# Cross attention with routed expert blocks: second transposes at the head of the next step, reciprocals spread through memory, product on GpSimd

## The chip, the cores and the metric

The kernel runs on one core of one Trainium2 chip. The metric is the device time of one execution in microseconds, as the median of several executions. A core has TensorE (PE, with its weight loads as PEld), VectorE (DVE), ScalarE (ACT), GpSimd (POOL) and SyncE (SP), which here only issues DMAs. Each runs its own list of instructions in order. The lists meet at semaphores: an instruction waits until a count is reached, and everything behind it on its engine waits too.

## What is computed

x is 128 sequences of 64 tokens of width 128, ctx the same shape. Cut to what matters:

```python
q = split_heads(layernorm(x) @ Wq.T + bq)          # 16 heads of 8
k = split_heads(ctx @ Wk.T + bk); v = split_heads(ctx @ Wv.T + bv)
probs = softmax(q @ k.T / sqrt(8))                 # within a sequence: 64 x 64
x = x + merge_heads(probs @ v) @ Wo.T + bo
xf = layernorm(x)
e = argmax(xf @ Wr.T + br)                         # one of 8 experts for each token
h = relu(xf @ W1[e].T + b1[e])                     # 128 -> 512
out = x + h @ W2[e].T + b2[e]
```

## The kernel before

The 8192 tokens are 64 tiles of 128 (two sequences a tile), in 16 groups of four tiles. There are three stages.

Stage 1 loads x and ctx group by group, normalises, and makes Q, K and V with TensorE; Q and K are kept with channels in the partitions (QT, KT). For the scores, K must be laid out block-diagonally: KM holds, for one group, each head's 8 channels in its own column block, zeros elsewhere. SP fills it by 16 small DMAs a group (line 341), with a buffer for each of two groups; for group 0 GpSimd does (line 410).

Stage 2 is a hand-made pipeline of steps. Step n works on several tiles at once, each at another stage:

- TensorE: scores of tile n (L877, banks 0 to 3, two tiles in turn); transposes of the exponentials of tile n-2 in two halves (L918), both into bank 4, the second half after other work of the step; between them the spreading matmul of tile n-8 (L948), the output matmul of tile n-9 (L952), in even steps the router's logits (L959), in odd steps the transposes of two finished tiles of X (L977, bank 6); then, for tile n-3, probabilities times values (L994, into bank 6) and the softmax denominators (L1003, into bank 5, a group's four tiles in one area).
- VectorE: the routing operations of a batch of eight tiles in a few steps of eight (L655 to L690), maximum over the scores (L698), once in four steps the reciprocal of a group's denominators (L702), subtraction (L706), the product of numerators and spread reciprocals (L722), the residual (L725), statistics for the second layer norm (L735 and the lines 587 to 595).
- ScalarE: numerators of tile n-4 to NUM (L526), first half of PT (L529), X1T in odd steps (L535), second half of PT (L538), the exponential of tile n (L546).
- GpSimd: two masked copies of V, VP, for tile n-1 (L451), the inverse root by Newton steps for batches 0 to 5, and one indirect DMA a step that sends a finished tile's rows to its experts' places (L466).

The reciprocals of a group lie in one 128x128 tile RD. To multiply them with one tile's numerators they must be spread over the eight channels of each head; L948 does this by a matmul with a 0/1 matrix C_SEL, into bank 7, from where VectorE reads them. The semaphores that matter: pt_done and pt_ready (each half of the transposes, each copy), exp_done, x1t_ready, rd_done, ot_ready. The matmuls L994 wait for the X1T copy of their step, since that copy reads bank 6, which they write.

Stage 3 runs 71 blocks of 128 rows through their expert (L1009 to L1037 on TensorE) and sends the rows home by indirect DMAs (L473). It begins at step 67, beside the last steps of the pipeline, which run on to the end of the routing. SOON says how many steps earlier than the others the last two batches are routed; L_MUL and L_X1 are the steps by which the product and the residual stand behind the scores.

Of the kernel before, what the change touches and what calls it, by code (L numbers as in the profile page):

```python
# [14 lines left out]
P = 128  # L15
D = 128
SEQ = 64
BATCH = 128
TOK = BATCH * SEQ
NT = TOK // P  # L20
GT = 4
NG = NT // GT
GW = GT * P
H = 16
# [20 lines left out]
C_ID, C_TRI, C_ONE, C_OWN, C_DEN, C_SEL, C_PREF, C_BASE, C_LIM, C_BLK, C_EPS, C_1H, C_LE, C_END = np.cumsum(  # L45
    [0, P, P, P, 2 * DK, GT * 64, GT * P, E, E, NT, NB, 1, ST, E * E]).tolist()
# [5 lines left out]
def constants():  # L52
# [12 lines left out]
    for t in range(GT):  # L65
        c[:, C_SEL + P * t:C_SEL + P * (t + 1)] = (p[:, None] // DK == p[None, :] // DK) & (p[:, None] % DK == t)
# [16 lines left out]
L_MUL = 8  # L83
L_X1 = 9
# [14 lines left out]
SOON = 2  # L99
# [67 lines left out]
def build(nc, x, ctxT, wts, we, w2, con, pad, ids, out):  # L167
# [3 lines left out]
    rows = nc.dram_tensor("rows", (ROWS, RW), f32).ap()  # L171

    ctx = ExitStack()
    with ctx:
# [20 lines left out]
        BQK = W[:, W_BQ:W_BQ + 2]  # L195
        WR, BR = W[:, W_R:W_R + E], W[:, W_BR:W_BR + E]

        X1T = sb("X1T", P, 4, 2, P)
# [37 lines left out]
        RD = sb("RD", P, 2, P)  # L236
        OT = sb("OT", P, 2, P)
# [37 lines left out]
        con_in, w_in, ids_in, w2_in = sem("con_in"), sem("w_in"), sem("ids_in"), sem("w2_in")  # L275
# [15 lines left out]
        num_kept, rdx_done, wr_mm, wr_ready = (sem(n) for n in ("num_kept", "rdx_done", "wr_mm", "wr_ready"))  # L291
# [19 lines left out]
        def _(sp):  # L311

            def load_group(s):
                def go(before):
# [3 lines left out]
                    if isinstance(s.n, int) and s.n == 0:  # L318
                        sp.dma_start(C[:], con).then_inc(con_in, 16)
                        sp.dma_start(W[:], wts).then_inc(w_in, 16)  # L320
                        sp.dma_start(IDS[:], ids).then_inc(ids_in, 16)
# [10 lines left out]
            def spread(s):  # L332
                sp.wait_ge(q_kept, s.n + 1)
                sp.sem_inc(spread_go, 1)
                need(sp, s_done, GT * (s.n - 1))
                sp.sem_inc(spread_go, 1)
                at = bass.ds(s.n * GW, GW)
                for g in range(2):
                    for j in range(HP):
                        own = slice(SEQ * g + DK * j, SEQ * g + DK * (j + 1))  # L340
                        sp.dma_start(KM[own, s.r, j, :], KT[own, at]).then_inc(km_in[s.r], 16)
            steps(sp, 1, NG, 2, spread, peel=2)


            for r in range(2):
                sp.wait_ge(km_in[r], 16 * H * (NG // 2 - 1 + r))
            sp.dma_start(PADR[:], pad).then_inc(padr_in, 16)
            sp.dma_start(WE[:], we).then_inc(we_in, 16)
            sp.wait_ge(s_done, NT - GT)
            sp.dma_start(W2, w2).then_inc(w2_in, 16)  # L350
# [18 lines left out]
            for n in range(NB1 - E):  # L369
# [727 lines left out]
```

## Time and profile before

| | us |
|---|---|
| median of 3 executions | 499.29 (499.02 to 500.56) |
| the profiled execution | 501.58, its span 499.8 |
| TensorE busy (weight loads) | 461.1, 92% (347.9, 70%) |
| VectorE busy | 408.2, 82% |
| ScalarE busy | 313.0, 63% |
| GpSimd busy | 240.6, 48% |
| granted TensorE clock, mean | 0.982 |

The span is the time between the first and the last record of the execution; the rest of its 501.58 us lies around it. Busy time is work recorded on the engine, and says nothing of whether the work was on the path. TensorE's matmuls are pipelined, so a group's duration reaches beyond the start of the next one: the distance between starts is what a group takes in the queue. An idle time is put down to the releaser that the semaphores name.

### The profile page before, as it was taken

What the parts mean: (1) busy time and instruction counts of PE and PEld (TensorE: products, weight loads), DVE (VectorE), ACT (ScalarE), POOL (GpSimd) and SP (SyncE); (2) the same over time, 40 slices, a digit from 0 to 9 for tenths busy, and PEclk for the clock granted to TensorE, in tenths of its full rate; (3) what the DMA queues carried; (4) which work ended last, traced back from release to release, by engine and by line L of the source; (5) the groups of instructions that cost most, each with busy time, mean ns of one, the idle gap of its engine ahead of it and who ended that gap; (6) DMA issues with size and microseconds to landing.
All of it is one profiled execution on the core that took longest, in us unless ns stands there. A gap on an engine that the chain in (4) does not pass through costs nothing. (4 is left out here: it accounts for less than half of the span.)

```text
span 499.8 us, 18728 instructions
## 1 busy us (share of the span) xinstructions
PE 461.1 (92%) x6467; PEld 347.9 (70%) x6467; DVE 408.2 (82%) x1061; ACT 313.0 (63%) x589; POOL 240.6 (48%) x390
## 2 busy tenths in 40 slices
PE   3999978899999999999999999988789999999990
PEld 1666634456666666666666666668779999999990
DVE  4999864677899899998999999958878887887870
ACT  1677764666666666666666665665557777777760
POOL 1548620222232464555645645554767645455551
PEclk9999995999999999999999999999999999999996
DMA  8356300011000111111111115722223332222100
GB/s 281 108 148 177 90 11 12 14 22 20 18 17 18 33 41 30 38 38 36 35 34 33 39 41 201 264 71 76 77 66 103 101 87 66 72 61 74 39 32 0
DMA packets 32752, 33.98 MB, mean 68 GB/s; under 512 B 6675, under 2 KB 26006, under 8 KB 32416
## 3 DMA queue, kind: packets, MB, share of 16 engines
q1 hardware_dynamic: 27840, 24.10, 18.7%
q0 software_dynamic: 4832, 8.80, 5.3%
q8 instruction: 53, 0.87, 0.8%
q14 instruction: 27, 0.22, 0.2%
HBM read 19.14 MB, written 9.99 MB: 58 GB/s over the span
## 5 line engine op out<-in xcount | busy, mean ns | idle before, releaser
L451 POOL TENSOR_TENSOR VP<-BIG,C 128x128 f32<-128x128 f32 x128 | 56.1, 458 | 136.5 <-PE PS L1003 132.7
L918 PEld LDWEIGHTS PS<-C,SB 128*128 128x128 f32 x512 | 54.6, 142 | 68.2 <-ACT SB L546 32.5
L698 DVE TENSOR_REDUCE MX<-PS 128x16 f32<-128x1024 f32 x64 | 78.3, 1223 | 29.1 <-PE PS L877 27.7
L473 POOL DMA_INDIRECT out<-SB,BIG x71 | 70.1, 987 | 52.6 <-DVE SB L849 44.7
L918 PE MATMUL PS<-C,SB 128*128 128x128 f32 x512 | 85.1, 290 | 7.5 <-ACT PT L529 7.2
L546 ACT ACTIVATE SB<-SB 128x1024 f32<-128x1024 f32 x64 | 67.7, 1057 | 23.7 <-DVE SB L706 22.0
L706 DVE TENSOR_TENSOR SB<-PS,MX 128x1024 f32<-128x1024 f32 x64 | 77.4, 1210 | 1.7
L1024 PE MATMUL PS<-BIG,KM 128*128 128x128 f32 x568 | 76.8, 277 | 0.3 <-issue 0.2
L1037 PE MATMUL PS<-KM,SB 128*128 x568 | 75.8, 277 | 0.6 <-ACT SB L563 0.6
L466 POOL DMA_INDIRECT rows<-X,DESTI x64 | 64.2, 1003 | 19.6 <-issue 14.1
L877 PE MATMUL PS<-KM,BIG 64*64 64x512 f32 x512 | 71.2, 629 | 0.8 <-ACT BIG L517 0.8
L559 ACT COPY KM<-BIG 128x644 f32 x71 | 51.7, 729 | 30.2 <-PE PS L1024 24.8
L1024 PEld LDWEIGHTS PS<-BIG,KM 128*128 128x128 f32 x568 | 69.7, 192 | 1.4 <-issue 1.2
L1037 PEld LDWEIGHTS PS<-KM,SB 128*128 128x128 f32 x568 | 69.1, 192 | 1.2 <-issue 0.8
L538 ACT COPY PT<-PS 128x512 f32<-128x512 f32 x64 | 37.5, 586 | 36.7 <-PE PS L918 36.6
L529 ACT COPY PT<-PS 128x512 f32<-128x512 f32 x64 | 37.4, 585 | 36.2 <-PE PS L918 32.8
L838 DVE TENSOR_TENSOR SB<-PS,KM 128x512 f32<-128x512 f32 x71 | 49.0, 690 | 5.4 <-PE PS L1024 2.4
L563 ACT ACTIVATE SB<-SB 128x512 f32<-128x512 f32 x71 | 44.6, 628 | 10.0 <-DVE SB L838 9.7
L994 PE MATMUL PS<-PT,VP 128*32 128x64 f32 x2048 | 42.3, 223 | 0.2
L1003 PE MATMUL PS<-PT,C 128*32 128x128 f32 x1024 | 40.3, 276 | 1.1 <-DVE RD L702 0.7
L994 PEld LDWEIGHTS PS<-PT,VP 128*32 128x32 f32 x2048 | 31.9, 110 | 11.1 <-issue 11.0
L846 DVE TENSOR_TENSOR SB<-PS,KM 128x128 f32<-128x128 f32 x71 | 20.6, 291 | 18.1 <-PE PS L1037 17.2
(122 smaller groups left out, 699.0 us busy)
## 6 DMA issues: line engine op xcount, KB each, us to landing
BIG<-rows SPq DMA_DIRECT2D x71, 66.0 KB, 1.9
X<-in_x SPq DMA_DIRECT2D x16, 256.0 KB, 3.3
PT<-in_ctxT SPq DMA_DIRECT2D x16, 256.0 KB, 3.0
KM<-BIG SPq DMA_DIRECT2D x240, 16.0 KB
BIG<-in_we SPq DMA_DIRECT2D x1, 2576.0 KB, 11.5
KM<-in_w SPq DMA_DIRECT2D x1, 2048.0 KB, 15.9
out<-SB,BIG POOLq DMA_INDIRECT x71, 2.3
rows<-X,DESTI POOLq DMA_INDIRECT x64, 2.4
```

The source lines that it names most:

```text
L451: last = nc.gpsimd.tensor_tensor(dst, v, own, ALU.mult)
L466: nc.gpsimd.indirect_dma_start(out=rows, out_offset=bass.IndirectOffsetOnAxis(ap=DESTI[:, j % 2, t:t + 1], axis=0), in_=X[:, j * ST + t, : ...
L473: nc.gpsimd.indirect_dma_start(out=out, out_offset=bass.IndirectOffsetOnAxis(ap=RT[:, s.r, ID:ID + 1].bitcast(i32), axis=0), in_=YO[:, s.r ...
L546: nc.scalar.activation(SB[:, n % 3, :], SB[:, n % 3, :], ACT.Exp, scale=SCALE).then_inc(exp_done, 1)
L559: nc.scalar.copy(WS[:, s.r % 4, :], WE[:, bass.ds(ex, 1), :].rearrange("p e f -> p (e f)")).then_inc(ws_ready, 1)
L698: nc.vector.tensor_reduce(MX[:, n % 2, :], sc, axis=AX.X, op=ALU.max).then_inc(mx_done, 1)
L706: nc.vector.tensor_tensor(SB[:, n % 3].rearrange("p (h k) -> p h k", h=H), sc, MX[:, n % 2, :].unsqueeze(2).to_broadcast([P, H, SEQ]), ALU ...
L877: last = nc.tensor.matmul(bank(2 * (n % 2) + g)[SEQ * b:SEQ * (b + 1), :], QT[rows_g, n * P + SEQ * b:n * P + SEQ * (b + 1)], KM[rows_g, g ...
L918: last = nc.tensor.transpose(bank(4)[:, i * P:(i + 1) * P], SB[:, n % 3, hp * P:(hp + 1) * P], ident)
L994: nc.tensor.matmul(bank(6)[32 * c:32 * c + 32, at:at + SEQ], VP[:, m % 2, b, 2 * c + z, :], PT[:, m % 2, 2 * c + z, SEQ * b:SEQ * b + SEQ] ...
L1024: last = nc.tensor.matmul(bank(2 + b.r % 2)[:, c * P:(c + 1) * P], WS[:, b.r % 4, c * P:(c + 1) * P], XT[:, b.r % 2, :], start=True, stop= ...
L1037: last = nc.tensor.matmul(bank(4 + b.r % 2)[:, 0:D], HT[:, b.r % 2, c * P:(c + 1) * P], w, start=c == 0, stop=c == FC - 1)
```

## The change

Four things change in the steps, and some around them.

- The second half of a tile's transposes leaves step n (tile n-2) and stands at the head of step n+1, before the scores; ScalarE's copy of it moves to the head of its own step, before the numerators.
- The spreading matmul and C_SEL are gone. SP writes a group's reciprocals to memory (ratio) and reads them back spread over the partitions into RDX, both inside its loop over the groups, after the spreading of K.
- The product moves from VectorE to GpSimd, at the head of its step, and L_MUL from 8 to 9; L_X1 from 9 to 10, with all that hangs on it (X's transposes and X1T now fall into even steps, the logits into odd ones); SOON from 2 to 1.
- The heads' order of channels in Q and K is turned (ScalarE makes turned copies of WQ and WK before the first projection, BQK comes by two small DMAs), so that KM takes 8 DMAs a group and not 16.
- X1T has two buffers, not four; WE and W2 are loaded from ScalarE's queue in its softmax loop, in pieces of at most 2048 elements; the wait for W2 moves to the third block.

```diff
-L_MUL = 8
-L_X1 = 9
+L_MUL = 9
+L_X1 = 10
-SOON = 2
+SOON = 1
...
+            def ratios(g):
+                sp.wait_ge(rd_done, g + 1)
+                need(sp, rdx_in[g % 2], 16 * (g // 2))
+                sp.dma_start(ratio[g % 2], RD[:, g % 2, :]).then_inc(rd_out[g % 2], 16)
+                need(sp, ot_ready, GT * (g - 1))
+                sp.wait_ge(rd_out[g % 2], 16 * (g // 2 + 1))
+                of = ratio[g % 2].rearrange("(h a) q -> h a q", a=DK)[:, 0:GT, :].rearrange("h t q -> h (t q)")
+                sp.dma_start(RDX[:, g % 2].rearrange("p t q -> p (t q)"), of.unsqueeze(1).to_broadcast([H, DK, GT * P])).then_inc(rdx_in[g % 2], 16)
...
+            for s in range(1, NG):
...
+                for j in range(HP):
+                    sp.dma_start(KM[j:P:HP, s % 2, j, :], KT[j:P:HP, s * GW:(s + 1) * GW]).then_inc(km_in[s % 2], 16)
+                if s >= 2:
+                    ratios(s - 2)
...
             def masks(s):
+                m = s.n - L_MUL
+                if 0 <= m < NT:
+                    g, t = divmod(m, GT)
+                    pool.wait_ge(rdx_in[g % 2], 16 * (g // 2 + 1))
+                    pool.wait_ge(num_kept, m + 1)
+                    need(pool, wo_done, m - 1)
+                    nc.gpsimd.tensor_tensor(OT[:, m % 2, :], RDX[:, g % 2, t, :], NUM[:, m % 8, :], ALU.mult).then_inc(ot_ready, 1)
...
             def softmax(s):
                 n = s.n
+                if 3 <= n < NT + 3:
+                    act.wait_ge(pt_done, 2 * (n - 3) + 2)
+                    nc.scalar.copy(PT[:, (n - 3) % 2, 4:8, :].rearrange("p a b -> p (a b)"), bank(4)).then_inc(pt_ready, 1)
...
-                if 2 <= n < NT + 2:
-                    act.wait_ge(pt_done, 2 * (n - 2) + 2)
-                    nc.scalar.copy(PT[:, n % 2, 4:8, :].rearrange("p a b -> p (a b)"), bank(4)).then_inc(pt_ready, 1)
...
+                if n == NT - 6:
+                    for r in range(2):
+                        act.wait_ge(km_in[r], 16 * HP * (NG // 2 - 1 + r))
+                    act.dma_start(WE[:].rearrange("p e f -> p (e f)"), we.rearrange("p e f -> p (e f)"), max_dma_last_dim=2048).then_inc(we_in, 16)
+                if n == NT - 3:
+                    act.wait_ge(s_done, NT - GT)
+                    act.dma_start(W2.rearrange("p e c d -> p (e c d)"), w2.rearrange("p e c d -> p (e c d)"), max_dma_last_dim=2048).then_inc(w2_in, 16)
...
-                m = n - L_MUL
-                if 0 <= m < NT:
-                    dve.wait_ge(num_kept, m + 1)
-                    nc.vector.tensor_tensor(OT[:, m % 2, :], bank(7)[:, 0:P], NUM[:, m % 8, :], ALU.mult).then_inc(ot_ready, 1)
...
             def stage2(s):
                 n = s.n
+                m = n - 3
+                if 0 <= m < NT:
+                    pe.wait_ge(pt_ready, 2 * m + 1)
+                    transposes(m, 1)
...
-                m = n - L_MUL
-                if 0 <= m < NT:
-                    g, t = divmod(m, GT)
-                    pe.wait_ge(rd_done, g + 1)
-                    nc.tensor.matmul(bank(7)[:, 0:P], C[:, C_SEL + P * t:C_SEL + P * (t + 1)], RD[:, g % 2, :],
-                                     start=True, stop=True).then_inc(rdx_done, 1)
...
-                m = n - 2
-                if 0 <= m < NT:
-                    pe.wait_ge(pt_ready, 2 * m + 1)
-                    transposes(m, 1)
```

How the instructions stand on TensorE in a step with X's transposes in the middle of stage 2, from its scores on, before (L918 transposes, L948 spreading, L952 output, L977 X's transposes, L994 values, L1003 denominators):

```order
L877 MATMUL PS<-KM,BIG 64x512 x3
L918 MATMUL PS<-C,SB 128x128 [waits pt_ready,exp_done]
L918 MATMUL PS<-C,SB 128x128 x3
L948 MATMUL PS<-RD,C 128x128 [waits rd_done,ot_ready,x1_done]
L952 MATMUL PS<-W,OT 128x128
L977 MATMUL PS<-C,X 128x128 [waits num_kept]
L977 MATMUL PS<-C,X 128x128
L918 MATMUL PS<-C,SB 128x128 [waits pt_ready]
L918 MATMUL PS<-C,SB 128x128 x3
L994 MATMUL PS<-PT,VP 32x64 [waits num_kept,x1t_ready,vp_done,pt_ready]
L994 MATMUL PS<-PT,VP 32x64 x15
L1003 MATMUL PS<-PT,C 32x128 x8
```

The same stretch now (L906 scores, L947 transposes, L980 output, L1005 X's transposes, L1018 values, L1027 denominators):

```order
L906 MATMUL PS<-KM,BIG 64x512 x3
L947 MATMUL PS<-C,SB 128x128 [waits pt_ready,exp_done]
L947 MATMUL PS<-C,SB 128x128 x3
L980 MATMUL PS<-W,OT 128x128 [waits ot_ready,x1_done]
L1005 MATMUL PS<-C,X 128x128 [waits num_kept]
L1005 MATMUL PS<-C,X 128x128
L1018 MATMUL PS<-PT,VP 32x64 [waits num_kept,x1t_ready,vp_done,pt_ready]
L1018 MATMUL PS<-PT,VP 32x64 x15
L1027 MATMUL PS<-PT,C 32x128 x8
L947 MATMUL PS<-C,SB 128x128 [waits pt_ready]
L947 MATMUL PS<-C,SB 128x128 x3
L906 MATMUL PS<-KM,BIG 64x512 [waits sub_done]
```

The second transposes stand behind the denominators, and nothing but L1005 now lies between the X transposes and the values that wait for x1t_ready.

ScalarE, such a step and the head of the following one, before (L526 NUM, L529 and L538 the halves of PT, L535 X1T, L546 exponential):

```order
L526 COPY NUM<-PS 128x128 [waits ot_ready,od_done]
L529 COPY PT<-PS 128x512 [waits pt_done]
L535 COPY X1T<-PS 128x256 [waits lgp_done,xt2_done]
L538 COPY PT<-PS 128x512 [waits pt_done]
L546 ACTIVATE SB<-SB 128x1024 [waits sub_done]
L526 COPY NUM<-PS 128x128 [waits ot_ready,od_done]
```

And now (L550 second half of PT, L554 NUM, L557 first half, L563 X1T, L571 exponential):

```order
L550 COPY PT<-PS 128x512 [waits pt_done]
L554 COPY NUM<-PS 128x128 [waits ot_ready,od_done]
L557 COPY PT<-PS 128x512 [waits pt_done]
L563 COPY X1T<-PS 128x256 [waits lgp_done,xt2_done]
L571 ACTIVATE SB<-SB 128x1024 [waits sub_done]
L550 COPY PT<-PS 128x512 [waits pt_done]
```

The copy of the second half stood before the exponential of its step; now it stands behind it, at the head of the next.

SP's queue in the middle of stage 2 now (L355 spreading of K, L343 reciprocals out, L347 back):

```order
L355 DMA KM<-BIG 16x512 [waits q_kept,s_done]
L355 DMA KM<-BIG 16x512 x7
L343 DMA ratio<-RD 128x128 [waits rdx_in1,rd_done]
L347 DMA RDX<-ratio 128x1x512 [waits rd_out1,ot_ready]
L355 DMA KM<-BIG 16x512 [waits q_kept,s_done]
```

Before, it held sixteen spreading DMAs of 8x512 a group and nothing between. A group's spreading now stands behind the two transfers of an earlier group's reciprocals.

## Rows read from the trace of the kernel before

**Rows 1.** Windows: stretch, length, busy us (instructions) of each engine, clock, DMA, GB/s.

```profile
70.80:75.60 4.80, 2.58 (x20) 0.85 (x20) 4.37 (x4) 2.17 (x3) 0.00 (x0) 0.96 0.00 0
75.60:85.90 10.30, 9.16 (x79) 4.50 (x80) 3.83 (x4) 4.34 (x7) 0.86 (x2) 0.52 0.06 11
200.00:232.00 32.00, 31.87 (x581) 21.35 (x576) 30.02 (x64) 20.31 (x36) 17.68 (x37) 1.00 0.15 35
```

**Rows 2.** Timeline, 230 to 237 us: start, duration, engine, line [idle before, releaser].

```profile
230.48 0.51 PE L959 MATMUL PS<-W,X1T 128*128 128x8 f32 x4
230.87 0.66 PE L918 MATMUL PS<-C,SB 128*128 128x128 f32 x4
...
232.48 1.09 PE L877 MATMUL PS<-KM,BIG 64*64 64x512 f32 x8
233.50 0.66 PE L918 MATMUL PS<-C,SB 128*128 128x128 f32 x4
233.64 1.23 DVE L698 TENSOR_REDUCE MX<-PS 128x16 f32<-128x1024 f32 x1 [0.88 <-PE PS L877]
233.99 0.39 PE L948 MATMUL PS<-RD,C 128*128 128x128 f32 x2
234.19 0.58 ACT L529 COPY PT<-PS 128x512 f32<-128x512 f32 x1 [0.79 <-PE PS L918]
234.22 0.39 PE L952 MATMUL PS<-W,OT 128*128 128x128 f32 x2
234.44 0.38 PE L977 MATMUL PS<-C,X 128*128 128x128 f32 x2
234.83 0.66 PE L918 MATMUL PS<-C,SB 128*128 128x128 f32 x4
234.86 0.37 ACT L535 COPY X1T<-PS 128x256 f32<-128x256 f32 x1
234.90 1.23 DVE L706 TENSOR_TENSOR SB<-PS,MX 128x1024 f32<-128x1024 f32 x1
235.42 0.65 PE L994 MATMUL PS<-PT,VP 128*32 128x64 f32 x32
235.89 0.62 PE L1003 MATMUL PS<-PT,C 128*32 128x128 f32 x16
236.15 1.06 ACT L546 ACTIVATE SB<-SB 128x1024 f32<-128x1024 f32 x1
236.44 1.09 PE L877 MATMUL PS<-KM,BIG 64*64 64x512 f32 x8
237.12 0.25 ACT L526 COPY NUM<-PS 128x128 f32<-128x128 f32 x1
```

**Rows 3.** Waits, 136 to 264 us: who <- for whom: total us, times, longest.

```profile
DVE MX L698 <- PE PS L877: 4.3, 8, 0.9
PEld PS L918 <- ACT PT L529: 3.9, 16, 0.2
```

**Rows 4.** Timeline of VectorE, a step with a reciprocal.

```profile
225.72 1.23 DVE L698 TENSOR_REDUCE MX<-PS 128x16 f32<-128x1024 f32 x1
226.86 0.95 DVE L702 RECIPROCAL RD<-PS 128x128 f32<-128x128 f32 x1
```

**Rows 5.** Groups by line, 136 to 264 us: busy us, mean ns | idle before.

```profile
L451 POOL TENSOR_TENSOR VP<-BIG,C 128x128 f32<-128x128 f32 x64 | 28.0, 457 | 56.0 <-PE PS L1003 56.0
L722 DVE TENSOR_TENSOR OT<-PS,NUM 128x128 f32<-128x128 f32 x31 | 8.7, 280 | 0.0
```

**Rows 6.** DMA issues of the page: queue, count, KB each, us to landing.

```profile
BIG<-rows SPq DMA_DIRECT2D x71, 66.0 KB, 1.9
X<-in_x SPq DMA_DIRECT2D x16, 256.0 KB, 3.3
```

**Rows 7.** Timeline of SP's queue, 219 to 236 us and 303 to 307 us.

```profile
219.10 17.17 SPq L341 DMA_DIRECT2D KM<-BIG  x17
...
304.40 1.57 SPq L348 DMA_DIRECT2D BIG<-in_we  x1
```

## What the change will do, as it was predicted

> **What bounds the kernel now.** I read the windows first, then the timeline of two middle steps, then the waits. Three stages follow each other: loading and projecting (to 68 us), attention in 67 steps (68 to about 335 us), the expert blocks (to 490 us). The change works almost only on the attention steps. There, over eight steps from 200 to 232 us, TensorE is busy 31.87 of 32.00 us and VectorE 30.02 [rows 1]: 4.00 us a step, and TensorE's own row leaves it no gap to speak of.
>
> The timeline of an odd step (these turn X's rows today; the change shifts that to the even ones) shows that this is partly cover [rows 2]. Scores start at 232.48 and last to 233.50 (1.02). The first four transposes start there; the copy of their result to PT starts at 234.19 and ends at 234.77, and only at 234.83 do the second four start, since both halves share bank 4. That round trip is 1.33 us, of which the transposes are 0.49, the spreading matmul L948 0.23, L952 0.22 and the two X transposes about 0.25: 1.19 of work and a wait of 0.25 at its end. After it come 0.59 to L994, 0.47 to L1003 and 0.55 to the next scores: 1.02 + 1.33 + 0.59 + 0.47 + 0.55 = 3.96, the measured distance (236.44 - 232.48). In an even step L959 (230.48 to 230.87, 0.39) fills the round trip. **So L948 costs nothing today**: without it the round trip would still be 1.33. In all, the wait for the PT copy is 3.9 us in 32 steps on TensorE's weight loads [rows 3], 0.12 a step.
>
> **The move of the transposes.** It takes the round trip away: the second half now runs at the head of the next step, when its copy has long been possible. Were TensorE alone, an odd step would be 0.50 (second half) + 1.02 + 0.49 + 0.22 (output matmul) + 0.39 (logits) + 0.09 + 0.47 + 0.55 = 3.73, an even one with 0.25 in place of 0.39 3.59. But three other orders now end last.
>
> First, X1T. In every even step from 12 on, the matmuls of probabilities and values wait for x1t_ready (they write the bank which that copy reads; the order of the changed kernel shows this wait). Before, the second transposes lay between. Now ScalarE copies the first PT half first: it starts 0.69 after the first transposes (234.19 - 233.50), X1T can start at the earliest 0.50 later and takes 0.37 [rows 2]. So the values start 1.62 after the first transposes instead of 1.05: 0.57 of wait. An even step has 1.02 + 1.62 + 0.47 + 0.55 + 0.50 = 4.16. Even and odd average 3.95: **this alone eats the whole gain.**
>
> Second, the exponentials. ScalarE's order is now: second PT copy of tile n-3, NUM, first PT copy, X1T, exp(n). The second copy at the head of step n+1 thus stands behind exp(n). From the start S of the scores of step n: the maximum starts at S + 1.16, the subtraction at S + 2.42, exp at S + 3.67 (236.15 - 232.48), and what follows exp starts 0.97 after it (237.12) [rows 2]: the copy runs from S + 4.64 to S + 5.22, and the first transposes of step n+1, which need bank 4 empty, start no earlier than S + 5.28. After an odd step TensorE is there at S + 3.73 + 1.02 = S + 4.75, and waits 0.53. From those transposes to the scores of step n+2 (even step's tail) it is 1.62 + 0.47 + 0.55 + 0.50 = 3.14. The loop over two steps is 5.28 + 3.14 = 8.42, or 4.21 a step; with the 0.08 that may stay between second transposes and what follows, 4.25.
>
> Third, the reciprocals. Every fourth step, always an odd one, VectorE puts one between maximum and subtraction: it starts 1.14 after the maximum and takes 0.95 [rows 4]. It lengthens the loop just described by about 0.87 (0.95 less overlap). The denominators' first matmul of the next group also waits for it: TensorE is there at S + 2.68, the reciprocal ends at S + 1.16 + 1.14 + 0.95 = S + 3.25; the 0.6 lies inside the 0.87. Per step 0.87/4 = 0.22. Routing steps add some 0.03.
>
> 4.25 + 0.22 + 0.03 = 4.50 at most, 4.43 at least; I take 4.47, where the same carrying of starts through the queues gives 4.0 for the old order, as measured. The reason that VectorE can't work ahead is that TensorE is late with scores: its own work is 30.02 - 8 x 0.28 (the product, L722 [rows 5]) = 27.8 in eight steps, 3.5 a step, so **removing the product brings nothing either**. Loss: 0.47 x 55 steps (12 to 66) = 25.9, less 0.8 for the steps before 12, which have no X1T copy: **+25 us**.
>
> **The product on GpSimd, the reciprocals through memory.** A two-input 128x128 operation takes GpSimd 0.457, and it is idle for 56.0 us of 32 steps, waiting for TensorE [rows 5]; per step it has 0.87 of masks, about 1.0 of an indirect DMA issue and now 0.46. It makes the product of step n one step before TensorE uses it. The transfers: 64 KB out (a 66 KB one took 1.9) and 256 KB back (a 256 KB one took 3.3) [rows 6], 5.2 together, 6 with the issues. A reciprocal is there at S + 3.3 of step 4g+7; the product is needed by TensorE in step 4g+10, 3 x 4.47 + 1.5 = 14.9 after S. 14.9 - 3.3 - 6 - 0.5 leaves 5.1 us of cover. Cost 0; it costs from the point where the two transfers take over 11 us. SP's queue is moved past, too: spreading K for group g+3 now stands behind them. Eight issues instead of sixteen, at most 1.0 us each (17.17 us for 17, waits included) [rows 7], start about 2.5 after the reciprocal: 3.3 + 2.5 + 8 + 3 of landing = 17 after S of step 4g+7, needed at step 4g+12, 5 x 4.47 = 22. Hidden. Without that cover each microsecond late would cost a microsecond per group.
>
> **Start and end.** C is 256 KB smaller, two tiny transfers for BQK and two ScalarE copies before the first projection come in: -1.0 to +0.5, taken as -0.5. The loads of WE and W2 are issued by ScalarE inside its softmax steps; SP took 1.57 for the first issue [rows 7]. ScalarE's copies are now on the loop, so 0 to +2.5, taken as +1. In steps 67 to 71, where L948 is not hidden by a round trip: 5 x 0.22 = -1.1. One routing step more in the blocks' stage: 0 to 0.6, +0.3. The moments and the seed of a batch fall into one VectorE step; they lie there back to back, no more work. Sum: -0.3.
>
> **The sum** against the profiled execution: 501.6 + 25 - 0.3 = 526.3. That execution is 2.3 above the median of 499.3, so 524.
>
> **Rivals.** (A) Faster: the two copies and exp are overlapped so well that TensorE's queue is the bound, (3.73 + 3.59)/2 + 0.03 = 3.69 a step, 0.31 x 55 = 17 less: 482. For it speaks that TensorE and the PT wait stand last today; against it, that the order of ScalarE is fixed and the rows leave 5.28 between scores and the transposes behind exp. It decides if X1T's copy ended less than 1.05 after the first transposes. 0.10. (B) No change: only the X1T wait binds, 3.95 and 0.03 of routing, 3.98 a step: 498. 0.06. (C) The loop binds at 4.25 but the reciprocal's 0.87 is taken up by slack from VectorE working ahead: 0.25 x 55 = 14: 513. 0.14. (D) The transfers come late, above all while WE and W2 load (4.6 MB in the same span): 3 us late in each of 16 groups would be +48, 570; a single late group only 3 to 8. 0.04. (E) The clock. From 70.8 to 75.6 TensorE was busy 2.58 of 4.80 us, and then ran at a granted 0.52 (1.2 GHz instead of 2.4) until 85.9 [rows 1]; work was about doubled there. In the new steps it idles 0.7 to 0.8 of 4.47, in pieces of 0.5 to 1.4. Each such 10 us stretch costs about 5: two or three make 534 to 539. 0.10. The Trainium skill (TensorE: Matmul & The Clock Gate, "A second HAM failure mode: psum-queue depth-cycling") says that short idle spells between groups of matmuls can be enough to make the clock go back and forth; by that rule (E) would be the likeliest; the trace agrees only for the one long idle spell, and in the blocks' stage no fall is seen before the end.
>
> **Chances.** Forecast as worked out (about 517 to 533): 0.56; C 0.14, A 0.10, E 0.10, B 0.06, D 0.04. The range takes in the forecast, C with its bounds and most of E: 508 to 537, leaving out A, B, D, about 0.2. Low end: C less 4 for the start and the issues; high end: 4.55 a step, +30, plus one clock stretch. Faster by over 0.3% (about what a measurement of this kernel can tell from no change) 0.10, within 0.06, slower 0.84.
>
> **What would show it.** Distance of scores in the middle near 4.47 on average, uneven: after an odd step a wait of the first transposes on the second PT copy, around 0.5; a wait of the values' matmuls on X1T around 0.6 in each even step; a wait of the denominators on the reciprocal every fourth step; ScalarE's PT copies waiting little for TensorE's second half; VectorE's share falling from 94% to about 80%; GpSimd's product waiting for no transfer. I am wrong if the steps are 4.0 or shorter, if those two copies are not what ends TensorE's idle time, or if RDX is waited for.

## The result, and the profile after

| | us |
|---|---|
| median of 4 executions, changed kernel | 534.05 (532.90 to 537.14) |
| median of 4 executions, kernel before, same chip | 499.15 (497.95 to 500.56) |
| ratio, 95% interval | 1.0694 [1.0652, 1.0737] |
| the profiled execution | 532.9, its span 531.1 |
| granted TensorE clock, mean | 0.986 |

The change costs 34.9 us by the medians and 31.3 by the two profiled executions (that of before lay 2.4 above its median, that of after 1.2 below). The forecast was 524, the range 508 to 537.

The page's engine rows: busy us, share of the span, instructions. Nearly the same work in a longer span: TensorE's and VectorE's busy time lies some 10 us below that of before, GpSimd's 24 above.

```profile
PE 450.9 (85%) x6339; PEld 337.4 (64%) x6339; DVE 397.7 (75%) x997; ACT 309.4 (58%) x591; POOL 264.2 (50%) x446
```

Windows after (columns as in [rows 1]): the pipeline's filling, eight middle steps from a score to a score, and a stretch early in the expert blocks.

```profile
68.00:90.00 22.00, 16.61 (x252) 7.96 (x248) 14.66 (x13) 12.71 (x21) 4.30 (x10) 1.00 0.05 14
200.00:236.80 36.80, 30.90 (x569) 20.06 (x561) 28.78 (x55) 19.93 (x38) 21.24 (x46) 1.00 0.16 49
362.00:372.00 10.00, 7.90 (x69) 7.45 (x58) 6.01 (x22) 6.09 (x12) 3.02 (x5) 0.68 0.34 90
```

The middle row answers to the third of [rows 1]: eight steps take 36.8 us, **4.60 a step** against 4.00 there (over 32 steps the old distance is 4.02), and TensorE is busy 84% instead of all of it. The distances from score to score repeat every eight steps: 3.78, 5.08 (positions of a routing batch), 4.46 (reciprocal), 4.85, 3.78, 4.85, 5.14 (moments, seed and reciprocal), 4.85. Every second step turns X's rows and takes 4.85 or more.

The timeline of two steps of after, an X step and the next, with columns as in [rows 2]. Lines: L906 scores, L947 transposes, L550 and L557 the copies of the second and first half to PT, L563 that of X1T, L1018 values, L1027 denominators, L730, L739 and L571 maximum, subtraction, exp.

```profile
224.05 0.63 PE L947 MATMUL PS<-C,SB 128*128 128x128 f32 x4 [0.48 <-ACT PT L550]
224.51 0.39 PE L980 MATMUL PS<-W,OT 128*128 128x128 f32 x2
224.71 0.59 ACT L557 COPY PT<-PS 128x512 f32<-128x512 f32 x1 [0.64 <-PE PS L947]
224.73 0.38 PE L1005 MATMUL PS<-C,X 128*128 128x128 f32 x2
225.19 0.38 ACT L563 COPY X1T<-PS 128x256 f32<-128x256 f32 x1
...
225.71 0.65 PE L1018 MATMUL PS<-PT,VP 128*32 128x64 f32 x32 [0.60 <-ACT X1T L563]
226.16 0.65 PE L1027 MATMUL PS<-PT,C 128*32 128x128 f32 x16
226.74 0.66 PE L947 MATMUL PS<-C,SB 128*128 128x128 f32 x4
227.32 1.09 PE L906 MATMUL PS<-KM,BIG 64*64 64x512 f32 x8
...
228.48 1.22 DVE L730 TENSOR_REDUCE MX<-PS 128x16 f32<-128x1024 f32 x1 [0.97 <-PE PS L906]
...
229.74 1.22 DVE L739 TENSOR_TENSOR SB<-PS,MX 128x1024 f32<-128x1024 f32 x1
...
231.00 1.06 ACT L571 ACTIVATE SB<-SB 128x1024 f32<-128x1024 f32 x1 [1.37 <-DVE SB L739]
231.11 1.09 PE L906 MATMUL PS<-KM,BIG 64*64 64x512 f32 x8
231.96 0.57 ACT L550 COPY PT<-PS 128x512 f32<-128x512 f32 x1
...
232.67 0.63 PE L947 MATMUL PS<-C,SB 128*128 128x128 f32 x4 [0.48 <-ACT PT L550]
```

Follow the loop: scores at 227.32, maximum 228.48, subtraction 229.74, exp 231.00 to 232.06. Behind exp on ScalarE stands the copy of the second half (231.96), and behind that the first transposes of the next step (232.67), 5.35 after the scores. Both halves share bank 4, so TensorE could go no further, though the next scores had been done since 232.20. From first transposes to the scores after next it is 3.27 (224.05 to 227.32). Two steps cost 5.35 + 3.27 = 8.62.

Waits of after, 208 to 280 us (columns as in [rows 3]):

```profile
ACT SB L571 <- DVE SB L739: 19.3, 16, 2.7
DVE MX L730 <- PE PS L906: 12.3, 11, 2.0
...
PE PS L1018 <- ACT X1T L563: 4.1, 7, 0.6
PEld PS L1027 <- DVE RD L735: 3.9, 4, 1.3
PE PS L947 <- ACT PT L550: 3.8, 8, 0.5
PE PS L1027 <- DVE RD L735: 3.3, 4, 1.2
```

Before, over the 32 steps of [rows 3], none of TensorE's matmuls has a row among the waits; its weight loads wait 3.9 us for a PT copy, and ScalarE waited for VectorE less than half as long in twice the steps:

```profile
ACT SB L546 <- DVE SB L706: 9.0, 12, 1.1
```

Now three engines wait in a circle: VectorE for the scores, ScalarE for VectorE, TensorE for ScalarE.

Where the 31.3 us lie, by the start of the same work in both traces:

| | before | after | difference |
|---|---|---|---|
| scores of step 0 | 67.89 | 68.44 | +0.6 |
| scores of step 12 | 116.24 | 112.63 | -3.6 |
| scores of step 20 | 148.19 | 148.89 | +0.7 |
| scores of step 63 | 321.74 | 346.63 | +24.9 |
| first expert block | 337.31 | 363.14 | +25.8 |
| block 18 | 383.70 | 414.82 | +31.1 |
| last block | 483.01 | 514.50 | +31.5 |

Three parts, then: a gain while the pipeline fills, a loss of 0.56 us in each of the 51 steps from 12 to 63 (28.5), and 5.3 in the first expert blocks.

**The gain** is the clock, and nothing shows that the change earned it. Before, TensorE ran at a granted 0.52, the lower level of 1.2 GHz, from 75.6 to 85.9 [rows 1]; after, the first window above shows 1.00 for 68 to 90 us. Yet the stretch ahead of it is the same in both traces: a wait of 2.67 us for the first PT copy, and TensorE busy 2.58 of 4.80 us. That of after:

```profile
71.30:76.10 4.80, 2.58 (x20) 0.85 (x20) 4.39 (x4) 2.13 (x4) 0.00 (x0) 1.00 0.00 0
```

Once the lower level followed and once it didn't. The variant with the moments early, below, has the changed kernel's start, and its clock fell there too (0.50 from 77.5 to 80).

**The blocks.** The last group's product on GpSimd comes late:

```profile
357.27 8.23 SPq L375 DMA_DIRECT2D BIG<-rows  x8
...
362.57 0.96 DVE L735 RECIPROCAL RD<-PS 128x128 f32<-128x128 f32 x1 [0.65 <-PE PS L1027]
...
365.19 0.46 PE L980 MATMUL PS<-W,OT 128*128 128x128 f32 x2 [1.75 <-DVE PREF L687]
...
365.60 0.38 SPq L343 DMA_DIRECT2D ratio<-RD  x1
...
367.38 0.55 SPq L347 DMA_DIRECT2D RDX<-ratio  x1
...
370.70 0.45 POOL L455 TENSOR_TENSOR OT<-RDX,NUM 128x128 f32<-128x128 f32 x1 [5.80 <-DMA RDX<-ratio]
```

The reciprocal is ready at 363.5, but SP has eight row loads ahead of the store, 8.23 us of issues. The store goes out at 365.60, the spreading load 1.78 later, and the product starts at 370.70: 7.2 after the reciprocal ended, 5.1 of it from the store on. But TensorE shows no wait for that product in this trace, and only 1.1 us in all for later ones of the group (379.98 and 382.92). It stood 1.75 us, up to 365.19, for VectorE's part of the routing logits (PREF); then it ran at the lower level (granted 0.50 from 366 to 372, 0.68 over the third window above); and at 374.03 it waits 0.94 for the routing positions. The kernel before waits 0.95 and 1.13 us in the same two places, and its clock stays at 1.00. So the late product and the 5.3 us stand side by side here. That the one makes the other isn't shown for this kernel.

### The profile page after: what moved, and what is told of

Read it like the earlier page. It is cut to its first block and busy times, and to the rows that moved or that the text cites. A ratio compares the mean times of both kernels' runs of the same rounds, so it can differ in the third digit from the quotient of the medians.

```text
span 531.1 us, 18142 instructions
## 1 busy us (share of the span) xinstructions
PE 450.9 (85%) x6339; PEld 337.4 (64%) x6339; DVE 397.7 (75%) x997; ACT 309.4 (58%) x591; POOL 264.2 (50%) x446
## 5 line engine op out<-in xcount | busy, mean ns | idle before, releaser
L730 DVE TENSOR_REDUCE MX<-PS 128x16 f32<-128x1024 f32 x64 | 78.4, 1224 | 61.4 <-PE PS L906 56.6
L571 ACT ACTIVATE SB<-SB 128x1024 f32<-128x1024 f32 x64 | 67.7, 1057 | 74.6 <-DVE SB L739 74.6
L947 PEld LDWEIGHTS PS<-C,SB 128*128 128x128 f32 x512 | 53.7, 141 | 87.0 <-ACT SB L571 49.5
L947 PE MATMUL PS<-C,SB 128*128 128x128 f32 x512 | 83.0, 285 | 22.1 <-ACT PT L550 19.4
L1048 PE MATMUL PS<-BIG,KM 128*128 128x128 f32 x568 | 78.9, 281 | 0.2
L739 DVE TENSOR_TENSOR SB<-PS,MX 128x1024 f32<-128x1024 f32 x64 | 77.4, 1209 | 1.7
L1048 PEld LDWEIGHTS PS<-BIG,KM 128*128 128x128 f32 x568 | 71.5, 196 | 1.4 <-issue 1.4
L906 PE MATMUL PS<-KM,BIG 64*64 64x512 f32 x512 | 69.5, 614 | 0.8 <-ACT BIG L542 0.8
L557 ACT COPY PT<-PS 128x512 f32<-128x512 f32 x64 | 37.5, 586 | 46.1 <-PE PS L947 46.1
L1018 PE MATMUL PS<-PT,VP 128*32 128x64 f32 x2048 | 41.9, 222 | 16.5 <-ACT X1T L563 16.5
L1027 PE MATMUL PS<-PT,C 128*32 128x128 f32 x1024 | 40.8, 274 | 10.6 <-DVE RD L735 10.6
L1018 PEld LDWEIGHTS PS<-PT,VP 128*32 128x32 f32 x2048 | 32.3, 109 | 24.3 <-ACT PT L557 21.5
L550 ACT COPY PT<-PS 128x512 f32<-128x512 f32 x64 | 36.9, 576 | 10.5 <-PE PS L947 10.4
```

The costliest lines, as they stand in the source:

```text
L571: nc.scalar.activation(SB[:, n % 3, :], SB[:, n % 3, :], ACT.Exp, scale=SCALE).then_inc(exp_done, 1)
L730: nc.vector.tensor_reduce(MX[:, n % 2, :], sc, axis=AX.X, op=ALU.max).then_inc(mx_done, 1)
L739: nc.vector.tensor_tensor(SB[:, n % 3].rearrange("p (h k) -> p h k", h=H), sc, MX[:, n % 2, :].unsqueeze(2).to_broadcast([P, H, SEQ]), ALU ...
L906: last = nc.tensor.matmul(bank(2 * (n % 2) + g)[SEQ * b:SEQ * (b + 1), :], QT[rows_g, n * P + SEQ * b:n * P + SEQ * (b + 1)], KM[rows_g, g ...
L947: last = nc.tensor.transpose(bank(4)[:, i * P:(i + 1) * P], SB[:, n % 3, hp * P:(hp + 1) * P], ident)
L1018: nc.tensor.matmul(bank(6)[32 * c:32 * c + 32, at:at + SEQ], VP[:, m % 2, b, 2 * c + z, :], PT[:, m % 2, 2 * c + z, SEQ * b:SEQ * b + SEQ] ...
```

## Experiments

All are edits of the changed kernel unless it says otherwise. Ratios are to the kernel before, with 95% intervals, on the same chip. "Step" is the mean distance of scores from step 20 to 52 in the profiled execution (before 4.02, after 4.60).

### Taking the move of the transposes out, and making it alone

In the first, the second half's transposes and their copy go back to their old place; all else of the change stays.

```diff
                 n = s.n
-                m = n - 3
-                if 0 <= m < NT:
-                    pe.wait_ge(pt_ready, 2 * m + 1)
-                    transposes(m, 1)
...
+                m = n - 2
+                if 0 <= m < NT:
+                    pe.wait_ge(pt_ready, 2 * m + 1)
+                    transposes(m, 1)
                 m = n - 3
```

> The changed kernel with the second half of the transposes back in its old place (between the X transposes and the values) and its PT copy back behind X1T; the transfers, the product on GpSimd and all else stay. Theory (the loss is made by the new place of the second half): steps fall from 4.60 us back to about 4.1 to 4.2, the waits of the values on X1T and of the first transposes on the second copy go, 505 to 512 us. Rival (the loss is made by the transfers, SP's queue or the product on GpSimd): nearly nothing changes, 525 to 534 us.

Measured: 513.57 us (1.6 above the range expected), ratio 1.0319 [1.0242, 1.0395], step 4.16. The move is worth some 20 of the 35 us. All steps are about 3.96 again but one in eight, and that one takes 5.55, against 4.25 in the kernel before: the one in which VectorE does moments, seed and reciprocal. The line of the denominators from 160 to 300 us (count, then busy us, mean ns, and idle before with its releaser), and one of its waits:

```profile
L1027 PE MATMUL PS<-PT,C 128*32 128x128 f32 x544 | 21.2, 273 | 5.5 <-DVE RD L735 5.5
```

```profile
211.66 0.64 PE L1027 MATMUL PS<-PT,C 128*32 128x128 f32 x16 [1.39 <-DVE RD L735]
```

The prediction had put this bunching at nothing. The second experiment is the mirror image: the kernel **before** with only the transposes and their copy moved (the diff read the other way).

> The kernel before with the second half of the transposes and its PT copy at the head of the next step, and nothing else changed. Theory: it alone makes most of the loss, steps of about 4.45, 518 to 526 us. Rival (the new place gains the hidden round trip, and the rest of the change loses): under 499 us.

Measured: 525.42 us, ratio 1.0507 [1.0438, 1.0575], step 4.42. The two agree: the move costs 3.7 to 5.1%, by itself or beside the rest. Its waits, 160 to 300 us:

```profile
PEld PS L918 <- ACT SB L546: 30.3, 32, 1.2
...
PE PS L994 <- ACT X1T L538: 8.9, 16, 0.6
...
PE PS L918 <- ACT PT L525: 3.4, 12, 0.4
```

X1T is waited for 0.6 in each of 16 steps, as forecast. The first row looks larger than it is: weight loads of the transposes stand there while the scores run, 0.95 a time, and before the change they did so for 0.8.

### One link of the loop at a time

Four edits, each on one of the waits above.

ScalarE's copy of the second half ahead of exp:

```diff
-                if 3 <= n < NT + 3:
-                    act.wait_ge(pt_done, 2 * (n - 3) + 2)
-                    nc.scalar.copy(PT[:, (n - 3) % 2, 4:8, :].rearrange("p a b -> p (a b)"), bank(4)).then_inc(pt_ready, 1)
...
+                if 2 <= n < NT + 2:
+                    act.wait_ge(pt_done, 2 * (n - 2) + 2)
+                    nc.scalar.copy(PT[:, n % 2, 4:8, :].rearrange("p a b -> p (a b)"), bank(4)).then_inc(pt_ready, 1)
                 if n < NT:
```

> The changed kernel with ScalarE's copy of the second half one place earlier: ahead of the exponential of the step before, not behind it. TensorE's order stays. Theory (the copy waits behind the exponential, and with it the next first transposes): the first transposes wait for it no more, steps of about 4.4, 517 to 526 us. Rival (only X1T and the reciprocals cost): no change within 3 us of 534.

Measured: 527.48 us (1.5 above the range expected), ratio 1.057 [1.0507, 1.0634], step 4.59. The wait of the first transposes is gone and an ordinary pair of steps fell from 8.63 to 8.24 (3.78 + 4.46), yet three of the four pairs at a seed between steps 20 and 52 rose from 9.99 to 11.5 or 11.6 (such as 5.81 + 5.75). Most of that is the clock. In those three TensorE's clock fell behind a wait of 1.7 us for the reciprocal; in the fourth, behind the same wait, it stayed at 1.00, and that pair took 10.18. Windows in one of the three, and over the fourth:

```profile
218.00:221.00 3.00, 3.00 (x14) 1.33 (x14) 1.11 (x3) 1.70 (x3) 2.59 (x8) 0.50 0.37 117
...
286.00:296.00 10.00, 7.72 (x139) 4.83 (x138) 8.83 (x20) 4.75 (x9) 6.98 (x20) 1.00 0.18 58
```

The new order can account for the rest: exp(n) now stands behind a copy that waits for TensorE to reach the head of step n+1.

```profile
ACT PT L568 <- PE PS L947: 32.9, 16, 3.6
```

That is ScalarE in 208 to 280 us: when TensorE is held up by the denominators, the copy and exp behind it are held up too, and ScalarE stands idle for up to 3.6.

In steps with X's transposes, denominators ahead of the values, so that what needs no X1T runs while it is copied:

```diff
-                    values()
-                    last = denominators()
+                    if turned:
+                        denominators()
+                        last = values()
+                    else:
+                        values()
+                        last = denominators()
```

> The changed kernel with the denominators ahead of the values in the steps that transpose X, so that the X1T copy has 0.47 us more to finish before bank 6 is written. Theory (the values' wait of 0.6 us in every second step is on the path): most of it goes, steps of about 4.4, 519 to 528 us. Rival (the loop through the exponential ends last anyway): the wait moves to the first transposes and the time stays within 3 us of 534.

Measured: 525.39 us, ratio 1.0523 [1.0465, 1.0582], step 4.47. The ordinary X step fell from 4.85 to 4.32 and the wait for X1T is 0.0 in the groups by line. So X1T was a real link. Three of the four pairs at a seed again rose, to 11.0 or 11.1 (such as 5.74 + 5.38). Its timeline:

```profile
217.56 0.64 PE L1030 MATMUL PS<-PT,C 128*32 128x128 f32 x16 [1.75 <-DVE RD L735]
...
218.72 1.98 PE L906 MATMUL PS<-KM,BIG 64*64 64x512 f32 x8
```

The denominators wait longer for the reciprocal (1.75), and the scores behind them take 1.98 instead of 1.09: the granted clock is at its lower level there (mean 0.60 from 218 to 222 us). The fourth pair has the same wait of 1.75, a clock of 1.00 (from 253 to 259 us), and took 10.06, hardly more than the 9.99 of the changed kernel. So here the rise is the clock.

The reciprocal ahead of the maximum on VectorE:

```diff
-                if n < NT:
-                    dve.wait_ge(s_done, n + 1)
-                    nc.vector.tensor_reduce(MX[:, n % 2, :], sc, axis=AX.X, op=ALU.max).then_inc(mx_done, 1)
                 g, late = divmod(n - L_RD, GT)
...
+                if n < NT:
+                    dve.wait_ge(s_done, n + 1)
+                    nc.vector.tensor_reduce(MX[:, n % 2, :], sc, axis=AX.X, op=ALU.max).then_inc(mx_done, 1)
```

> The changed kernel with VectorE's reciprocal ahead of the maximum of its step, where VectorE waits for scores anyway. Theory (the reciprocal between maximum and subtraction lengthens the loop by its 0.87 or so every fourth step, and the denominators wait for it): the wait of the denominators goes, steps of about 4.5, 525 to 531 us. Rival (the reciprocal lies in slack): 532 to 536 us.

Measured: 538.73 us, ratio 1.0797 [1.0744, 1.0851], step 4.70: **slower**, where a gain was expected. The ordinary reciprocal step did fall, 4.46 to 3.78. But at the seed the pair rose from 9.99 to 11.43 (4.02 + 7.41). Scores of that step start at 216.77. VectorE, and TensorE's next first transposes:

```profile
217.69 0.68 DVE L777 TENSOR_SCALAR Y<-YY 128x8 int32<-128x8 int32 x1
...
218.41 0.17 DVE L779 TENSOR_SCALAR HALF<-VAR 128x8 f32<-128x8 f32 x1
...
218.62 0.96 DVE L732 RECIPROCAL RD<-PS 128x128 f32<-128x128 f32 x1
...
219.49 1.16 DVE L735 TENSOR_REDUCE MX<-PS 128x16 f32<-128x1024 f32 x1
...
223.62 0.63 PE L947 MATMUL PS<-C,SB 128*128 128x128 f32 x4 [1.74 <-ACT PT L550]
```

Moments, seed and reciprocal all stand before the maximum, which starts 2.72 after the scores instead of 1.85 in the changed kernel's seed step. That costs little, since there the reciprocal came behind the maximum: from the scores to the first transposes of the next step it is 6.85 here and 6.73 there (217.32 to 224.05). What changed is that TensorE's idle time lies in one piece of 1.74, not in two of 1.16 and 0.48. From those transposes to the following scores it is then 4.58 instead of 3.27, and there the clock is low. Windows of this kernel, in two places eight steps apart:

```profile
182.00:186.00 4.00, 2.27 (x31) 1.00 (x28) 3.93 (x6) 1.64 (x3) 3.35 (x11) 1.00 0.28 86
186.00:190.00 4.00, 3.36 (x58) 2.80 (x59) 2.30 (x7) 1.88 (x4) 1.01 (x5) 0.67 0.25 74
...
220.00:224.00 4.00, 2.26 (x28) 1.04 (x18) 3.93 (x6) 1.70 (x3) 3.43 (x10) 1.00 0.34 102
224.00:228.00 4.00, 3.40 (x59) 2.68 (x57) 1.88 (x7) 1.82 (x3) 1.07 (x5) 0.61 0.23 69
```

After each stretch in which TensorE idled 1.7 of 4 us, its granted clock fell to the lower level for a part of the next 4. This was rival E, seen here at each of six seeds, in the two variants above at four and at three, and not in the changed kernel's middle. By the pairs with and without a fall in those two variants (11.5 against 10.18, 11.12 against 10.06) one fall costs 1.1 to 1.4 us. Six of them make 6 to 8, an estimate, and this kernel is slower by 4.7. So the order by itself may well have gained what was expected, and lost it to the clock; that is estimated, not shown.

The moments of a batch one step before its seed, as the kernel before had them apart:

```diff
-M_BN = L_X1 + 1
+M_BN = L_X1
```

> The changed kernel with the statistics of the second norm taken in the step of the residual itself and no more a step later, so that a batch's moments fall one step ahead of the seed again, as in the kernel before. Theory (moments, seed and reciprocal in one VectorE step push maximum and reciprocal back by 0.7 us in every eighth step): that step falls from 5.14 to about 4.46, 527 to 531 us. Rival (they lie in slack): 532 to 536 us.

Measured: 530.6 us, ratio 1.0625 [1.0578, 1.0673], step 4.52. The seed's step fell from 5.14 to 4.53, the level of a plain reciprocal step; the others are unchanged.

### All of them together, and the control without the move

All four edits at once:

> The changed kernel with four repairs: copy of the second half ahead of the exponential, denominators first where X is transposed, reciprocal ahead of the maximum, statistics early. Theory (these four waits are what keeps the new place of the second half from paying): steps of about 3.95 to 4.1, 490 to 505 us, about as fast as the kernel before or faster. Rival (something else in the new order binds as well): above 512 us.

Measured: 497.47 us, ratio **0.9956 [0.9932, 0.998]**, step 3.94 (3.78, 3.93, 3.81, 4.49, 3.78, 4.03, 3.78, 3.93). The circle is broken. Its waits from 208 to 280 us have no row of TensorE for ScalarE or VectorE above 1.4 us in all; what leads them is ScalarE waiting for TensorE:

```profile
ACT PT L568 <- PE PS L947: 26.4, 18, 1.6
PEld PS L947 <- issue: 17.2, 28, 0.8
```

By the ratios, the four edits alone sum to 1.24 + 1.71 - 1.03 + 0.69 = 2.6% of the time before; together they give 7.4%. In a loop through several queues, shortening one link gives the others the turn. Not all of the gap between 2.6 and 7.4 is that, though. The first three single edits had 13 falls of the clock between 150 and 340 us in their profiled executions, by the estimate above 14 to 18 us or some 3% of the time, and the kernel with all four edits had none there (1.00 from 86 to 326 us). How much the loop alone makes wasn't separated.

The control has the transposes in their old place and the moments early, with all the rest of the change (reciprocals through memory, product on GpSimd):

> Both undone: second half in its old place and statistics early; the transfers, the product on GpSimd and the rest stay. Theory (these two are the whole loss, the transfers and the product are hidden and bring nothing): the step of 5.55 in every eight goes to about 4.0, 499 to 505 us. Rival (the transfers or SP cost something of their own): 508 us and more.

Measured: 505.67 us, ratio 1.0138 [1.0071, 1.0206], step 4.00. The middle costs what it did before, and step 63 starts 2.7 earlier than before (step 12 had been 3.1 earlier, by the clock as above); but block 18 starts 3.6 later. So what is left of the loss without the move lies wholly in the first blocks: from the first block to block 18 it is 52.8 us, 6.4 more than before. Its last group's product waits 7.33 for RDX, and here TensorE waits for that product, with the lower clock level behind it (0.57 from 345 to 349 us):

```profile
345.02 0.46 PE L976 MATMUL PS<-W,OT 128*128 128x128 f32 x2 [2.35 <-POOL OT L455]
```

With this run the two losses of the middle can be set side by side, each with and without the other, all else being the changed kernel: neither 1.0138, bunched moments alone 1.0319, move alone 1.0625, both 1.0694. The move costs 4.9% of the time before where the moments are early and 3.7% where they are bunched. The bunching costs 1.8% without the move and 0.7% with it. So the two overlap, and a single edit of the changed kernel, as that of the moments above, shows the smaller price.

### The last group's transfers

In the kernel with four edits and in the control, the last group's store and load go three row loads behind the start instead of eight:

```diff
-                if n == 8:
+                if n == 3:
                     ratios(NG - 1)
```

> The kernel with the four repairs, and the last group's reciprocals sent by SP behind three of the row loads of the first blocks, not behind eight. Theory (the product of the last group waits 5 to 7 us for them, while steps take only about 2.6 us, and TensorE and its clock lose with it): the wait shrinks by 2 to 4 us, 493 to 496 us against 497.5. Rival (the wait lies beside the blocks' work): 497 to 498 us.

> Second half in its old place, statistics early, and the last group's reciprocals behind three row loads. Theory: 2 to 4 us under the 505.7 of the same kernel with them behind eight, 501 to 504 us. Rival: 505 to 506 us.

Measured: 496.77 us, ratio 0.9949 [0.9919, 0.9979], and 503.52, ratio 1.0069 [1.0039, 1.0099]. The waits for RDX fell to 3.87 and 3.57, and in the profiled executions the stretch from the first block to block 18 from 52.1 to 50.3 and from 52.8 to 50.5 (before 46.4). The first misses its expected range by 0.8. The ratios of both pairs overlap within their intervals, so no more than some 2 us is claimed. Much of it can be the clock: both of these executions have 1.00 over that stretch, while the two with the transfers behind eight loads have some 3 us at the lower level, right behind a wait of TensorE for the product (1.86 and 2.35 us). Even at a clock of 1.00 the stretch is still some 4 us longer than before. In another kernel the control's last group goes without transfers: its last four tiles are multiplied by what RDX held before, not divided by their own denominators.

```diff
-                if n == 8:
-                    ratios(NG - 1)
...
+                    if g < NG - 1:
+                        pool.wait_ge(rdx_in[g % 2], 16 * (g // 2 + 1))
```

> Second half in its old place, statistics early, and the last group's transfers left out: its product uses what RDX holds and waits for nothing, so the last four tiles are not divided by their own denominators. This sizes the whole cost of the last group's transfers. Theory: the first 18 blocks take 47 to 48 us as in the kernel before and not 53, 499 to 502 us. Rival (the extra routing step or something else costs there): 504 us and more.

Measured: 502.86 us, ratio 1.0072 [1.0039, 1.0106], 2.8 below the control by the medians. So the late transfers are worth at most some 3 us; about as much over before stays in the blocks without them. One cause of that could be the additional routing step; it wasn't separated. In this kernel's profiled execution the clock was low for part of that stretch too (0.66 from 335 to 350), so its own trace settles nothing there.

### Is the rest of the change needed?

The kernel **before** with the move and three of the edits (copy ahead of exp, denominators ahead in X steps, reciprocal ahead of the maximum); spreading matmul and product stay where they were.

> The kernel before (spreading matmul and product on VectorE kept) with the second half at the head of the next step and three repairs: copy ahead of the exponential, denominators first where X is transposed, reciprocal ahead of the maximum. It says what the transfers and the product on GpSimd are worth once the new place is repaired. Theory (TensorE alone is then the bound, and L948's 0.22 us counts): steps of 4.05 to 4.1 against 3.94 with the transfers, but no late last group, 494 to 499 us. Rival (TensorE's matmul is still covered): steps of 3.95 or less, under 494 us.

Measured: 496.39 us, ratio **0.9947 [0.9918, 0.9976]**, step 4.02. The same as with the transfers and GpSimd's product. Those make the middle 0.08 a step shorter (3.94), about 4 us, and give it back in the blocks. Between first block and block 18 the profiled executions have 52.1 with them and 50.3 without, but the clocks differ: the 50.3 hold 10 us at a granted 0.53 (334 to 344 us), the 52.1 only some 3 us at 0.50. At full clock the 50.3 would be up to 5 us shorter, an estimate, and near the 46.4 of before; this execution indeed lay 5.4 above the kernel's median, at a mean clock of 0.975. By this estimate the transfers, the product and what else of the change lies in the blocks cost nearer 5 us there than 1.8. What the clock falls of the single executions do to the medians isn't known.

## Why the prediction was right in direction and too low

**The loop was read rightly.** Its three links are in the trace of after with nearly the lengths forecast: X1T is waited for 0.60 (0.57), the first transposes wait 0.48 for the second PT copy (0.53), from scores to those transposes it is 5.35 (5.28), from there to the scores after next 3.27 (3.14). In sum 8.62 for two steps, forecast 8.42 to 8.50. Two terms were short by about a tenth of a microsecond each, and over 55 steps a tenth a pair is nearly 3 us. The first two experiments show the cause: the move costs 5.1% on the kernel before, and 4.9% on the changed kernel with the moments early.

**The step that failed: "The moments and the seed of a batch fall into one VectorE step; they lie there back to back, no more work."** No more work is true, but the step in which they fall has the reciprocal too, and VectorE's order is on the loop. That step takes 5.14 where a plain reciprocal step takes 4.46: 0.68 every eighth step, 0.09 a step, 5 us in all. Pulling the moments out took 0.61 of it back, and 3.5 us by the medians (530.6 against 534.05). Without the move the same bunching costs 1.3 in that step, 5.55 against the 4.25 of the control, and 1.8% of the time before.

**The reciprocal was over-sized.** Forecast 0.87 each, measured 0.68 (4.46 - 3.78); 0.17 a step instead of 0.22. Denominators wait 0.47 for it, forecast 0.6, inside the same 0.68, and 1.16 in the seed's step. The sum a step: 4.31 (pairs) + 0.17 + 0.09 + 0.03 (positions) = 4.60, forecast 4.47.

**+25 at step 63 is partly luck.** The traces agree, 24.9, but as 28.5 of loss from step 12 on less 3.6 gained ahead of it, nearly all by the clock that did not fall, behind the same idle stretch. The forecast had -0.8 for those first steps and nothing for the clock. Other executions of before may hold less of that slow stretch: in the experiments they ran at mean clocks of 0.981 to 0.992, the profiled one at 0.982. That would fit the larger difference of 34.9 by the medians; their traces weren't taken.

**Behind the middle the forecast had almost nothing, and 6.4 came.** That is the size of rival D for a single group, 3 to 8 us. The cover of the transfers had been worked out for steps of 4.47 with SP's queue short; the last group's store falls into the blocks' loads, where eight issues of about 1.0 stand ahead of it and the steps are shorter. The transfer itself was sized right (5.1 after the store, forecast 5.2). Only up to 3 us of the stretch are shown to hang on it, in the variants; in the changed kernel's own trace TensorE waits 1.1 us in all for that group's products, and some 7 us of the stretch run at the lower clock level. The rest stays open.

**What held.** In the middle GpSimd's product waits for no transfer (in several variants one waits 1.1 to 3.4 us while the expert weights load), and VectorE is busy 28.78 of 36.80, 78% (forecast about 80). The start came 0.6 later instead of 0.5 earlier; the variants with the same start spread from 67.8 to 68.7, so that is within what it varies. The loads of the next weights took ScalarE's queue 0.44 and 0.39 us, near the 1 that was taken for both.

**The rivals.** A (steps of 3.69, 482): no. B and C (498, 513): no; the reciprocal is not taken up by slack. C's state can be made, though: with the reciprocal ahead of the maximum its step is 3.78. E did not decide the changed kernel; one stretch of some 7 us in the blocks shows it, and in the middle three experiments. The Trainium skill ("TensorE: Matmul & The Clock Gate", "A second HAM failure mode: psum-queue depth-cycling") warns that short gaps between groups of matmuls can make the clock go back and forth. The traces agree in part: waits of up to 1.16 every few steps left the clock at 1.00 in the changed kernel's middle; waits of 1.7 were followed by a fall in most places but not in all; and one of 2.67 was followed by a fall before and by none after.

## What to carry to other kernels

Moving work out of a round trip on one engine doesn't remove the round trip; ask where its copy now stands in the other engine's queue, and follow the loop over as many steps as its pattern has, here two. When a loop runs through three in-order queues, a single repair says little about its link: here single repairs gave 1.2, 1.7 and 0.7% and one lost 1.0%, all together 7.4%. Look at the granted clock before you explain such a difference by the order; three of the four had falls of it that the changed kernel's middle and the full repair had not. And price "the same work, bunched in one step" by the queue it stands in, and each cover in the stage where it is shortest.

## What the runs showed of the hardware

- The clock can fall for a few microseconds at a time and recurrently, and the same idle stretch isn't always followed by a fall (a wait of 2.67 us: yes before, no after; waits of 1.7: three of four seeds in each of two variants). With TensorE idle 1.7 of 4 us once in eight steps, the granted clock was 0.96 over 76 us in the variant with the reciprocal first:

```profile
160.00:236.00 76.00, 64.55 (x1158) 42.54 (x1162) 58.64 (x114) 40.16 (x74) 41.54 (x89) 0.96 0.15 47
```

- The same product of 128x128 takes 0.280 us on VectorE reading PSUM [rows 5] and 0.464 on GpSimd from SBUF (40 of them from 136 to 320 us):

```profile
L455 POOL TENSOR_TENSOR OT<-RDX,NUM 128x128 f32<-128x128 f32 x40 | 18.5, 464 | 1.0
```

- Spreading values through memory (64 KB out, 256 KB back) takes 5.1 us from the first issue to use, of which 1.8 passes before the second issue.
